# A graph layer with residual and layer norm on one core: GpSimd's statistics placed ahead of the next group's differences, one evacuation ahead of joins, three evacuations and four feature loads moved

## The chip, the core and the metric

The kernel runs on one core of a Trainium2 chip. The core has TensorE (PE, matrix multiply), VectorE (DVE), ScalarE (ACT), GpSimd (POOL) and SyncE (SP), which here only issues DMAs. Each engine works through its own queue in program order, and the queues meet at semaphores. The metric is device time of one launch in microseconds (us), the median of several runs; lower is better.

## The reference

```python
def _gcn_layer(x, adj, W, b):
    d_inv_sqrt = (jnp.sum(adj, axis=1) + 1e-09) ** (-0.5)
    msg = d_inv_sqrt[:, None] * adj * d_inv_sqrt[None, :] @ x
    return jax.nn.relu(msg @ W + b)
H_f = _gcn_layer(x, adj, W_f, b_f)            # x: 4096 x 128, adj: 4096 x 4096, fp32
H_s = _gcn_layer(spatial_x, adj, W_s, b_s)
attn = sigmoid(concat([H_f, H_s]) @ W_att + b_att)
x = x + attn * H_f + (1 - attn) * H_s
out = (x - mean(x)) / sqrt(var(x) + 1e-5)     # over the 128 features of a row
```

## The kernel before

Rows are cut into 32 tiles of 128; four tiles make a group, so there are 8 groups of output rows (512 each). The big product adj @ (D x) is taken in 64 items of four 128x512 blocks of the transposed adjacency (`raw`, 1 MB an item, three buffers; At is laid out on the host in the order of use). Each fp32 operand is split into a high and a low fp32r part: ACT writes the high part `Ah` (`high(k)`, L614), DVE the low part `Al` = raw - Ah (`low(k)`, L460), and likewise `Yh` (L642) and `Yl` (L471) for the scaled features. PE does three matmuls for a block and half (L377 to L379), 24 for an item, into one of four PSUM pairs; when a run of blocks ends, DVE evacuates the two halves of the pair into `acc` (`evacuate`, L479 or L482), and the next run on the same pair waits for that.

The degrees D need row sums of adj itself, which is loaded a second time in halves of 1 MB (`nat`, three buffers, `parts[k]` says before which item) and summed on ACT (L627); GpSimd turns sums into D (L723, L726) and, for the last two column groups, adds blocks of raw into column sums (L760). A load into `raw` waits for the low part three items back, one into `nat` for the row sum three halves back. SP issues all loads in one order written out by hand: for each item the halves of adj in `parts[k]`, the item's raw block, then feature loads (`load_x`, 0.5 MB each).

The last 16 items (FINAL = 48 to 63) end the product of one group after another: groups 0 to 6 end at items 50, 51, 53, 55, 57, 59 and 61, group 7 in two halves at 62 and 63. Each engine has the epilogue of a finished group at fixed items after its end (`L_MIX` 4, `L_JOIN` 5, `L_SQUARE` 6, `L_NORM` 7). For a group g:

- DVE evacuates it; PE multiplies it by the weights (`weigh(g)`, L387) behind the item after the group's last, and group 6 inside item 62;
- DVE `affine` (L496) and `logit` (L505); ACT `relu` (L649) and `gate` (sigmoid, L654);
- GpSimd `mix(r)` for each of the four tiles: the difference `fin` (L766) and residual plus H_s in `xs` (L767);
- DVE `join` (L513): xs += att * difference, with the row sum `ysum`;
- GpSimd `mean` (L772, `less`), ACT `square` (L658, with row sum `ysq`), GpSimd `deviation` (L777 vare, L780 rstd = power -0.5, L783 shift), ACT `normalise` (L663), SP stores the tile (L363).

On ACT, item k is: high(k), gate, normalise, square, relu, each where a group is due. On DVE it is: low(k), join, affine, logit, evacuations. Behind the loop both engines have the rest written out by hand. Group 7 goes in halves of two tiles (HALVES) with its statistics on DVE (`join_last`, `normalise_last`, L517 to L536) and the power on GpSimd (`last_deviation`, L788).

"Evacuation of 62" below is run 62, that is group 6; "high(63)" and "low(63)" are those of the last item. A count such as mix(1) or square(4) in the text is that of a group.

Of the kernel before, what the change touches and what calls it, by code (L numbers as in the profile page):

```python
# [13 lines left out]
GT = 4  # L14
# [53 lines left out]
def build(nc, At, adj, xs_in, W_f, W_s, b_f, b_s, W_att, b_att, out):  # L68
# [5 lines left out]
    G = T // GT  # L74
# [46 lines left out]
    FULL = (G - 2) * GT  # L121
    OWN_COLUMNS = 2 * G
    parts = {k: [] for k in range(K)}
    for k, r in [(0, 0), (1, 1), (4, 2), (5, 3), (8, 4), (9, 5), (10, 6), (11, 7)]:
        parts[k] = [2 * r, 2 * r + 1]
    for n, k in zip(range(16, 24), [13, 14, 15, 16, 16, 17, 17, 18]):
        parts[k].append(n)
    for n in range(24, 36):
# [18 lines left out]
        return sum(len(summed_blocks(i)) for i in range(k + 1))  # L147

    SHARED = [0, 1, 3]

    COLLECT = FINAL - 6

# [33 lines left out]
    with ExitStack() as ctx:  # L186
# [126 lines left out]
        @block.sync  # L313
        def _(sp):
            def load_item(k):
                if k >= RAWS:
                    sp.wait_ge(low_ok, GT * (k - RAWS + 1))
                    if summed_blocks(k - RAWS):
                        sp.wait_ge(block_sum_ok, blocks_summed(k - RAWS))
                if k == 1:  # L320
                    for i in range(GT):
                        sp.dma_start(raw[:, k, i * IB:(i + 1) * IB],
                                     At_v[k, :, i * IB:(i + 1) * IB]).then_inc(raw1_in[i], 16)
                else:
                    sp.dma_start(raw[:, k % RAWS, :], At_v[k]).then_inc(raw_in[k % RAWS], 16)

            def load_part(n):
                r = tile_of(n)
                if n >= NATS:
                    part_summed(sp, n - NATS)  # L330
                if r < FULL:
                    sp.dma_start(nat[:, n % NATS, :], adj_v[r, n % 2]).then_inc(nat_in[n % NATS], 16)
                else:
                    sp.dma_start(nat[:, n % NATS, :].rearrange("p (q c) -> p q c", q=2),
                                 adj_ends[r]).then_inc(nat_in[n % NATS], 16)

            def load_x(m):
                sp.dma_start(xs[:, m * GT:(m + 1) * GT, :], xs_v[m]).then_inc(xs_sem[m], 16)

            sp.dma_start(xs[:, 0:1, :], xs_v[0, :, 0:1, :]).then_inc(x_first, 16)  # L340
            for k in range(K):
                for n in parts[k]:
                    load_part(n)
                if k == 1:
                    sp.dma_start(xs[:, 1:GT, :], xs_v[0, :, 1:GT, :]).then_inc(xs_sem[0], 16)
                load_item(k)
                if k == 6:
                    load_x(1)
                if k % G == G - 1 and k // G + 2 < G:
                    load_x(k // G + 2)  # L350
                if k == 3 * G:
                    sp.dma_start(Wfs[:, 0:H], W_f).then_inc(const_in, 16)
                    sp.dma_start(Wfs[:, H:H2], W_s).then_inc(const_in, 16)
                    sp.dma_start(bias[:, 0:H], bf_v).then_inc(const_in, 16)
                    sp.dma_start(bias[:, H:H2], bs_v).then_inc(const_in, 16)
                    sp.dma_start(watt[:, :], watt_v).then_inc(const_in, 16)
                    sp.dma_start(batt[:, :], batt_v).then_inc(const_in, 16)
            for r in range(T):
                if r < LAST:
                    sp.wait_ge(norm_ok, r + 1)  # L360
                else:
                    sp.wait_ge(last_norm_ok, r - LAST + 1)
                sp.dma_start(out_v[r], xs[:, r, 0:F]).then_inc(stored, 16)  # L363
            sp.wait_ge(stored, 16 * T)
# [88 lines left out]
        def _(dve):  # L453
# [31 lines left out]
            def evacuate(e):  # L485
                evacuate_half(e, 0)
                evacuate_half(e, 1)
# [12 lines left out]
            def logit(r):  # L500
                dve.wait_ge(z_ok, r + 1)
                if r >= ZRING:
                    dve.wait_ge(logit_ok, r - ZRING + 1)
                c = (r % ZRING) * H2
                dve.scalar_tensor_tensor(out=nat[:, 1, c:c + H2], in0=z_of(r), scalar=0.0,  # L505
                                         in1=watt[:, :], op0=ALU.max, op1=ALU.mult,
                                         accum_out=lg[:, r:r + 1]).then_inc(logit_ok, 1)
# [25 lines left out]
            def normalise_last(r):  # L533
                dve.wait_ge(last_rstd_ok, r - LAST + 1)
                dve.tensor_scalar(xs[:, r, 0:F], xs[:, r, 0:F], mv[:, r, 0:1], rstd[:, r:r + 1],  # L535
                                  ALU.subtract, ALU.mult).then_inc(last_norm_ok, 1)  # L536

            def of_group(g):
                return range(g * GT, (g + 1) * GT)
# [10 lines left out]
            def evacuate_new(runs_ended):  # L550
                for e in runs_ended:
                    if e not in evacuated:
                        evacuated.add(e)
                        evacuate(e)

            for k in range(K):
                ended = [e for e in evac_order if end_item[e] == k - 2]
                evacuate_new(ended if k < 2 * G else ended[:1] if len(ended) == GT else [])
                if k == 1:
                    own_share(3)  # L560
                low(k)
                for r in y_at[k]:
                    if r >= PIECED:
                        y_low(r)
                g = group_at(k, L_JOIN)
                if g is not None:
                    for r in of_group(g):
                        join(r)
                g = group_at(k, L_MIX)
                if g is not None:  # L570
                    for r in of_group(g):
                        affine(r)
                    for r in of_group(g):
                        logit(r)
                if k < K - 1:
                    evacuate_new(ended)
            for r in of_group(TAIL - 2):
                join(r)
            evacuate(FIRST_LAST + TAIL - 1)
            evacuate_half(FIRST_LAST + TAIL, 0)  # L580
            for r in of_group(TAIL - 1):
                affine(r)
# [10 lines left out]
            for r in HALVES[0]:  # L593
                join_last(r)
            evacuate_half(FIRST_LAST + TAIL + 1, 1)
            for r in HALVES[0]:
                normalise_last(r)
            for r in HALVES[1]:
                affine(r)
                logit(r)  # L600
            for r in HALVES[1]:
                join_last(r)
            for r in HALVES[1]:
# [4 lines left out]
        def _(act):  # L608
# [47 lines left out]
            def square(r):  # L656
                act.wait_ge(less_ok, r + 1)
                act.activation(fin[:, r % ROWS, H_F], xs[:, r, 0:F], ACT.Square, bias=less[:, r:r + 1],  # L658
                               accum_out=ysq[:, r:r + 1]).then_inc(ysq_ok, 1)
# [6 lines left out]
            def of_group(g):  # L666
                return range(g * GT, (g + 1) * GT)

            for k in range(K):
                for n in parts[k]:  # L670
                    row_sum(n)
                high(k)
                if k == COLLECT + 3:
                    column_sums()
                for r in y_at[k]:
                    if r >= PIECED:
                        y_high(r)
                if k == FINAL:
                    act.wait_ge(const_in, 16 * 6)
                g = group_at(k, L_JOIN)  # L680
                if g is not None:
                    gate(of_group(g))
                g = group_at(k, L_NORM)
                if g is not None:
                    for r in of_group(g):
                        normalise(r)
                g = group_at(k, L_SQUARE)
                if g is not None and k < K - 1:
                    for r in of_group(g):
                        square(r)  # L690
                g = group_at(k, L_MIX)
                if g is not None:
                    for r in of_group(g):
                        relu(r)
            for r in of_group(TAIL - 3):
                square(r)
            gate(of_group(TAIL - 2))
            for r in of_group(TAIL - 3):
                normalise(r)
# [20 lines left out]
        def _(pool):  # L720
# [89 lines left out]
            def of_group(g):  # L810
                return range(g * GT, (g + 1) * GT)

            for g in range(TAIL):
                if g >= 1:
                    mean(of_group(g - 1))
                if g == TAIL - 1:
                    deviation(of_group(g - 1))
                for r in of_group(g):
                    mix(r)
                if 1 <= g < TAIL - 1:  # L820
                    deviation(of_group(g - 1))
            mean(of_group(TAIL - 1))
            for r in HALVES[0]:
                mix(r)
# [33 lines left out]
```

## Time and profile before

| | us |
|---|---|
| median of 3 runs | 418.4 (418.27 to 418.67) |
| the profiled execution's own time | 419.03 |
| its span (first to last instruction) | 417.2 |
| PE busy, share of the span | 375.0, 90% |
| DVE busy | 292.5, 70% |
| ACT busy | 284.5, 68% |
| GpSimd busy | 145.5, 35% |
| moved by DMA | 132.84 MB, 318 GB/s over the span |

PE has most of the span, but busy shares do not tell where time is lost. The rows below give start and length in us from the span's start; what stands in square brackets is how long the engine had been idle just before, and whose instruction ended that.

### The profile page before, as it was taken

The numbers are of one execution on the slowest core, as the hardware profiler recorded it, in microseconds if no ns is written. First come the engines' busy times: TensorE is split into PE (matmuls) and PEld (weight loads), VectorE is DVE, ScalarE is ACT, GpSimd is POOL, SyncE is SP. The second block draws the span as 40 slices with busy tenths as digits, with TensorE's granted clock in tenths as the row PEclk, the third lists the DMA queues.
The fourth block names the chain that finished last, engine by engine and source line by source line (L and its number), as shares of the span: only waits on it lengthen the run. The fifth ranks groups of instructions, "written<-read, shape, count | busy, mean of one in ns | idle before, by whom it ended". The sixth has DMA issues, their size and how long they took to land. (4 is left out here: it accounts for less than half of the span.)

```text
span 417.2 us, 5235 instructions
## 1 busy us (share of the span) xinstructions
PE 375.0 (90%) x1728; PEld 311.7 (75%) x1728; DVE 292.5 (70%) x407; ACT 284.5 (68%) x343; POOL 145.5 (35%) x194
## 2 busy tenths in 40 slices
PE   0679999689989998999989999999999999999492
PEld 0557887578868886888778877888888888887491
DVE  2569993496566966598654958489756996966776
ACT  3768588777887739877888677664433685574653
POOL 1203001000000791049211799342000557634574
PEclk9999999989999999999999999999999999999888
DMA  8999999999999989999999999897555535250001
GB/s 304 408 423 422 416 425 419 420 422 421 420 419 423 417 335 400 424 419 421 421 421 423 412 415 386 317 386 285 201 199 199 190 122 194 103 176 27 24 28 50
DMA packets 25530, 132.84 MB, mean 318 GB/s; under 512 B 2848, under 2 KB 7712, under 8 KB 11296
## 3 DMA queue, kind: packets, MB, share of 16 engines
q1 hardware_dynamic: 25504, 132.53, 79.4%
q8 instruction: 13, 0.21, 0.2%
q14 instruction: 13, 0.11, 0.1%
HBM read 130.42 MB, written 2.10 MB: 318 GB/s over the span
## 5 line engine op out<-in xcount | busy, mean ns | idle before, releaser
L377 PE MATMUL sums<-Ah,Yh 128*128 128x512 f32 (+1 forms) x528 | 206.0, 390 | 27.4 <-DVE Yl L471 18.8
L460 DVE TENSOR_TENSOR Al<-raw,Ah 128x2048 fp32r<-128x2048 f32 (+1 forms) x70 | 151.9, 2173 | 96.1 <-ACT Ah L614 95.1
L379 PE MATMUL sums<-Al,Yh 128*128 128x512 f32 (+1 forms) x528 | 204.0, 386 | 0.0
L378 PE MATMUL sums<-Ah,Yl 128*128 128x512 f32 (+1 forms) x528 | 203.9, 386 | 0.0
L614 ACT ACTIVATE Ah<-raw 128x2048 fp32r<-128x2048 f32 (+1 forms) x70 | 123.5, 1768 | 54.3 <-DMA raw<-in_At 29.0
L377 PEld LDWEIGHTS sums<-Ah,Yh 128*128 128x128 f32 x528 | 100.9, 191 | 50.4 <-DVE Yl L471 20.0
L627 ACT ACTIVATE nat<-nat 128x2048 f32<-128x2048 f32 x53 | 101.6, 1918 | 21.3 <-DMA nat<-in_adj 20.0
L379 PEld LDWEIGHTS sums<-Al,Yh 128*128 128x128 f32 x528 | 100.5, 190 | 19.7
L378 PEld LDWEIGHTS sums<-Ah,Yl 128*128 128x128 f32 x528 | 100.7, 191 | 19.1
L482 DVE TENSOR_TENSOR acc<-sums,acc 128x512 f32<-128x512 f32 (+1 forms) x114 | 71.8, 671 | 7.5 <-PE sums L379 7.3
L723 POOL TENSOR_SCALAR dg<-rs 128x1 f32<-128x1 f32 x22 | 11.3, 514 | 153.3 <-ACT nat L627 153.0
L760 POOL TENSOR_TENSOR S<-S,raw 128x512 f32<-128x512 f32 x32 | 58.6, 1832 | 8.2 <-DMA raw<-in_At 4.3
L766 POOL TENSOR_TENSOR fin<-fin 128x128 f32<-128x128 f32 x32 | 17.3, 541 | 64.7 <-ACT fin L649 64.7
L649 ACT ACTIVATE fin<-nat 128x256 f32<-128x256 f32 x32 | 12.6, 416 | 17.7 <-DVE nat L496 17.6
L387 PE MATMUL sums<-Wfs,acc 128*128 128x128 f32 x128 | 17.9, 296 | 6.9 <-DVE acc L482 6.8
L387 PEld LDWEIGHTS sums<-Wfs,acc 128*128 128x128 f32 x128 | 17.1, 209 | 8.1 <-DVE acc L482 7.7
L642 ACT ACTIVATE Yh<-xs,D 128x256 fp32r<-128x256 f32 x32 | 15.2, 494 | 11.1 <-POOL D L726 9.3
L663 ACT ACTIVATE xs<-xs,shift,rstd 128x128 f32<-128x128 f32 x28 | 11.5, 481 | 15.1 <-POOL shift L783 15.1
L471 DVE SCALAR_TENSOR_TENSOR Yl<-xs,D,Yh 128x256 fp32r<-128x256 f32 x32 | 18.4, 591 | 4.2 <-ACT Yh L642 4.2
L505 DVE SCALAR_TENSOR_TENSOR nat<-nat,watt 128x256 f32<-128x256 f32 x32 | 18.1, 614 | 0.1
L767 POOL TENSOR_TENSOR xs<-xs,fin 128x128 f32<-128x128 f32 x32 | 17.7, 553 | 0.0
L496 DVE SCALAR_TENSOR_TENSOR nat<-sums,D,bias 128x256 f32<-128x256 f32 x32 | 13.5, 475 | 2.9 <-PE sums L387 2.9
(45 smaller groups left out, 115.2 us busy)
## 6 DMA issues: line engine op xcount, KB each, us to landing
raw<-in_At SPq DMA_DIRECT2D x63, 1024.0 KB, 10.0
nat<-in_adj SPq DMA_DIRECT2D x56, 1024.0 KB, 11.5
xs<-in_xs SPq DMA_DIRECT2D x7, 512.0 KB, 11.2
out<-xs SPq DMA_DIRECT2D x32, 64.0 KB, 1.6
raw<-in_At SPq DMA_DIRECT2D x4, 256.0 KB, 9.7
xs<-in_xs SPq DMA_DIRECT2D x1, 384.0 KB, 9.2
xs<-in_xs SPq DMA_DIRECT2D x1, 128.0 KB, 2.4
watt<-in_W_att SPq DMA_DIRECT2D x1, 128.0 KB, 9.6
```

The lines of the kernel that those rows point to most:

```text
L377: pe.matmul(to, Yh[:, t % YRING, hs], high, start=first, stop=False)
L378: pe.matmul(to, Yl[:, t % YRING, hs], high, start=False, stop=False)
L379: mm = pe.matmul(to, Yh[:, t % YRING, hs], low, start=False, stop=last)
L387: return pe.matmul(sums[:, 3, bank, c + half * H:c + (half + 1) * H], acc[:, r // GT, half, q * P:(q + 1) * P], Wfs[:, half * H:(half + 1) ...
L460: dve.tensor_tensor(Al[:, k % SPLITS, a * IB:b * IB], raw[:, k % RAWS, a * IB:b * IB], Ah[:, k % SPLITS, a * IB:b * IB], ALU.subtract).the ...
L471: dve.scalar_tensor_tensor(out=Yl[:, r % YRING, :], in0=xs[:, r, :], scalar=D[:, r:r + 1], in1=Yh[:, r % YRING, :].bitcast(F32), op0=ALU.mult,
L482: dve.tensor_tensor(acc[:, g, half, a:b], sums[:, pair, half, 0:b - a], acc[:, g, half, a:b], ALU.add).then_inc(evac_ok, 1)
L505: dve.scalar_tensor_tensor(out=nat[:, 1, c:c + H2], in0=z_of(r), scalar=0.0, in1=watt[:, :], op0=ALU.max, op1=ALU.mult, accum_out=lg[:, r: ...
L614: act.activation(Ah[:, k % SPLITS, a * IB:b * IB], raw[:, k % RAWS, a * IB:b * IB], ACT.Copy).then_inc(high_ok, b - a)
L627: act.activation(nat[:, n % NATS, :], nat[:, n % NATS, :], ACT.Copy, accum_out=rs[:, r, h:h + 1]).then_inc(rs_act, 1)
L760: pool.tensor_tensor(S[:, g, :], S[:, g, :], raw[:, k % RAWS, j * IB:(j + 1) * IB], ALU.add).then_inc(block_sum_ok, 1)
L767: pool.tensor_tensor(xs[:, r, 0:F], xs[:, r, 0:F], f[:, H_S], ALU.add).then_inc(res_ok, 1)
```

## The change

Seven edits, none of which adds or drops an engine instruction:

1. SP and ACT: half 4 of adj is loaded and summed ahead of item 3, half 5 ahead of item 4 (both ahead of item 4 before).
2. SP: `load_x(2)` behind item 10 (was 7), `load_x(3)` behind 17 (15), `load_x(4)` behind 25 (23), `load_x(7)` behind 43 (47).
3. DVE: at items 17, 25 and 33 the run that ended two items earlier is evacuated ahead of the low part, not behind it.
4. DVE: the evacuation of 62 stands ahead of the joins of group 5.
5. DVE: `normalise_last` of the first half stands behind affine and logit of the second half.
6. ACT: the squares of group 4 stand in the loop at item 63, ahead of relu of group 5, not behind it.
7. GpSimd: `deviation(g-1)` stands ahead of `mix(g)` for all g, not only for g = 6.

(Edit 2 is four loads; the evacuations of edit 3 are of the runs that ended at items 15, 23 and 31.)

```diff
--- before.py
+++ after.py
@@ -121,8 +121,9 @@
     FULL = (G - 2) * GT
     OWN_COLUMNS = 2 * G
     parts = {k: [] for k in range(K)}
-    for k, r in [(0, 0), (1, 1), (4, 2), (5, 3), (8, 4), (9, 5), (10, 6), (11, 7)]:
+    for k, r in [(0, 0), (1, 1), (5, 3), (8, 4), (9, 5), (10, 6), (11, 7)]:
         parts[k] = [2 * r, 2 * r + 1]
+    parts[3], parts[4] = [4], [5]
     for n, k in zip(range(16, 24), [13, 14, 15, 16, 16, 17, 17, 18]):
         parts[k].append(n)
     for n in range(24, 36):
@@ -147,6 +148,8 @@
         return sum(len(summed_blocks(i)) for i in range(k + 1))
 
     SHARED = [0, 1, 3]
+    X_AFTER = {6: 1, 10: 2, 17: 3, 25: 4, 31: 5, 39: 6, 43: 7}
+    EVACUATE_FIRST = [k for k in range(K) if k < 2 * G or k in (17, 25, 33)]
 
     COLLECT = FINAL - 6
 
@@ -344,10 +347,8 @@
                 if k == 1:
                     sp.dma_start(xs[:, 1:GT, :], xs_v[0, :, 1:GT, :]).then_inc(xs_sem[0], 16)
                 load_item(k)
-                if k == 6:
-                    load_x(1)
-                if k % G == G - 1 and k // G + 2 < G:
-                    load_x(k // G + 2)
+                if k in X_AFTER:
+                    load_x(X_AFTER[k])
                 if k == 3 * G:
                     sp.dma_start(Wfs[:, 0:H], W_f).then_inc(const_in, 16)
                     sp.dma_start(Wfs[:, H:H2], W_s).then_inc(const_in, 16)
@@ -555,7 +556,7 @@
 
             for k in range(K):
                 ended = [e for e in evac_order if end_item[e] == k - 2]
-                evacuate_new(ended if k < 2 * G else ended[:1] if len(ended) == GT else [])
+                evacuate_new(ended if k in EVACUATE_FIRST else ended[:1] if len(ended) == GT else [])
                 if k == 1:
                     own_share(3)
                 low(k)
@@ -574,9 +575,9 @@
                         logit(r)
                 if k < K - 1:
                     evacuate_new(ended)
+            evacuate(FIRST_LAST + TAIL - 1)
             for r in of_group(TAIL - 2):
                 join(r)
-            evacuate(FIRST_LAST + TAIL - 1)
             evacuate_half(FIRST_LAST + TAIL, 0)
             for r in of_group(TAIL - 1):
                 affine(r)
@@ -593,11 +594,11 @@
             for r in HALVES[0]:
                 join_last(r)
             evacuate_half(FIRST_LAST + TAIL + 1, 1)
-            for r in HALVES[0]:
-                normalise_last(r)
             for r in HALVES[1]:
                 affine(r)
                 logit(r)
+            for r in HALVES[0]:
+                normalise_last(r)
             for r in HALVES[1]:
                 join_last(r)
             for r in HALVES[1]:
@@ -685,15 +686,13 @@
                     for r in of_group(g):
                         normalise(r)
                 g = group_at(k, L_SQUARE)
-                if g is not None and k < K - 1:
+                if g is not None:
                     for r in of_group(g):
                         square(r)
                 g = group_at(k, L_MIX)
                 if g is not None:
                     for r in of_group(g):
                         relu(r)
-            for r in of_group(TAIL - 3):
-                square(r)
             gate(of_group(TAIL - 2))
             for r in of_group(TAIL - 3):
                 normalise(r)
@@ -813,12 +812,9 @@
             for g in range(TAIL):
                 if g >= 1:
                     mean(of_group(g - 1))
-                if g == TAIL - 1:
                     deviation(of_group(g - 1))
                 for r in of_group(g):
                     mix(r)
-                if 1 <= g < TAIL - 1:
-                    deviation(of_group(g - 1))
             mean(of_group(TAIL - 1))
             for r in HALVES[0]:
                 mix(r)
```

## Rows read from the trace of the kernel before

**Rows 1.** Stretches: busy PE, PEld, DVE, ACT, POOL; clock, DMA share, GB/s.
```profile
160.00:250.00 90.00, 86.75 (x381) 70.84 (x379) 62.18 (x55) 72.99 (x65) 39.22 (x36) 1.00 1.01 420
290.00:350.00 60.00, 60.00 (x291) 50.58 (x290) 46.46 (x79) 31.89 (x50) 17.41 (x30) 1.00 0.52 187
```

**Rows 2.** PE's timeline (start, length, line; idle before), items 11, 16, 40.
```profile
84.58 0.50 PE L377 MATMUL sums<-Ah,Yh 128*128 128x512 f32 x1 [2.68 <-DVE Yl L471]
...
119.35 0.50 PE L377 MATMUL sums<-Ah,Yh 128*128 128x512 f32 x1 [1.58 <-DVE acc L482]
...
251.05 0.47 PE L377 MATMUL sums<-Ah,Yh 128*128 128x512 f32 x1 [1.38 <-issue]
```

**Rows 3.** ACT's and DVE's timeline ahead of item 40.
```profile
241.81 0.51 ACT L642 ACTIVATE Yh<-xs,D 128x256 fp32r<-128x256 f32 x1 [3.67 <-POOL D L726]
...
246.01 1.90 ACT L614 ACTIVATE Ah<-raw 128x2048 fp32r<-128x2048 f32 x1
...
248.05 2.90 DVE L460 TENSOR_TENSOR Al<-raw,Ah 128x2048 fp32r<-128x2048 f32 x1 [3.53 <-ACT Ah L614]
```

**Rows 4.** PE's timeline: the weights' products of groups 3, 5 and 6.
```profile
350.82 1.95 PE L387 MATMUL sums<-Wfs,acc 128*128 128x128 f32 x16
...
377.30 1.94 PE L387 MATMUL sums<-Wfs,acc 128*128 128x128 f32 x15 [0.96 <-DVE acc L482]
...
393.60 3.78 PE L387 MATMUL sums<-Wfs,acc 128*128 128x128 f32 x16 [5.88 <-DVE acc L482]
```

**Rows 5.** Stretches behind idle time of PE; clock behind POOL's count.
```profile
86.00:88.50 2.50, 2.50 (x8) 1.92 (x7) 2.50 (x4) 1.94 (x3) 0.00 (x0) 0.50 1.01 419
393.60:397.40 3.80, 3.80 (x18) 3.80 (x19) 1.16 (x3) 3.58 (x14) 0.52 (x2) 0.50 0.24 69
```

**Rows 6.** The list of waits (us in total, times, longest).
```profile
ACT xs L663 <- POOL shift L783: 15.1, 4, 4.3
```

**Rows 7.** ACT's timeline: normalise of group 3, high(63), normalise of group 4.
```profile
380.73 1.65 ACT L663 ACTIVATE xs<-xs,shift,rstd 128x128 f32<-128x128 f32 x4 [4.29 <-POOL shift L783]
382.29 1.90 ACT L614 ACTIVATE Ah<-raw 128x2048 fp32r<-128x2048 f32 x1
...
393.38 1.65 ACT L663 ACTIVATE xs<-xs,shift,rstd 128x128 f32<-128x128 f32 x4 [2.52 <-POOL shift L783]
```

**Rows 8.** DVE's timeline: low(57), evacuation, low(63), join, evacuation of 62, affine.
```profile
340.44 2.29 DVE L460 TENSOR_TENSOR Al<-raw,Ah 128x2048 fp32r<-128x2048 f32 x1 [0.88 <-ACT Ah L614]
...
346.37 1.28 DVE L482 TENSOR_TENSOR acc<-sums,acc 128x512 f32<-128x512 f32 x2
...
384.32 2.29 DVE L460 TENSOR_TENSOR Al<-raw,Ah 128x2048 fp32r<-128x2048 f32 x1 [3.75 <-ACT Ah L614]
...
390.90 0.44 DVE L513 SCALAR_TENSOR_TENSOR xs<-fin,att,xs 128x128 f32<-128x128 f32 x1 [0.42 <-ACT att L654]
...
392.27 1.61 DVE L482 TENSOR_TENSOR acc<-sums,acc 128x512 f32<-128x512 f32 x3
...
403.53 0.87 DVE L496 SCALAR_TENSOR_TENSOR nat<-sums,D,bias 128x256 f32<-128x256 f32 x2 [0.20 <-PE sums L387]
```

**Rows 9.** POOL's timeline: deviation of groups 0, 3 and 5, end of mix(6).
```profile
337.16 1.35 POOL L777 TENSOR_SCALAR vare<-ysq 128x4 f32<-128x4 f32 x1 [0.94 <-ACT fin L658]
...
377.50 2.87 POOL L780 TENSOR_TENSOR rstd<-vare,mhalf 128x4 f32<-128x4 f32 x1
...
396.73 0.20 POOL L777 TENSOR_SCALAR vare<-ysq 128x4 f32<-128x4 f32 x1 [3.23 <-ACT fin L658]
...
398.21 0.47 POOL L783 TENSOR_TENSOR shift<-less,rstd 128x4 f32<-128x4 f32 x1
...
402.12 0.51 POOL L767 TENSOR_TENSOR xs<-xs,fin 128x128 f32<-128x128 f32 x1
```

**Rows 10.** DVE's normalise_last of the first half; SP's last eight stores.
```profile
408.91 0.60 DVE L535 TENSOR_SCALAR xs<-xs,mv,rstd 128x128 f32<-128x128 f32 x2 [0.42 <-POOL rstd L788]
...
411.98 3.65 SPq L363 DMA_DIRECT2D out<-xs  x8
```

## The prediction, made before the changed kernel was run

> **What bounds the kernel now.** I read the table by stretches first. From 160 to 250 us DMA moves 420 GB/s with no slack (share 1.01) while PE is busy for 86.75 of 90 us; from 290 to 350 DMA moves 187 GB/s and PE is busy all the time [rows 1]. So there are two regimes: up to about item 40 the bytes set the pace and PE's pauses are its slack; from there PE sets it. PE's timeline shows those pauses: 2.68 us for Yl at item 11, 1.58 us for an evacuation inside item 16 (two more of that kind, 1.48 and 1.44 us, inside items 24 and 32), 1.38 us ahead of item 40 [rows 2]. Item 40 waited for its low part, 248.05 + 2.90 = 250.95, which waited for high(40) at 246.01, and ACT got to that late because it had waited 3.67 us for D ahead of two row sums [rows 3]. None of these waits is for PE. Third, the end: PE stands 0.96 us at the weights of group 5 and 5.88 us at those of group 6, both for an evacuation [rows 4], and runs at half clock behind the second (0.50, that is 1.2 GHz, from 393.6 to 397.4) [rows 5]. Why the evacuations are late is in ACT's rows: it waits four times, 15.1 us in all, for GpSimd's shift [rows 6]. One of these, 4.29 us, holds normalise of group 3 until 380.73, and high(63) stands behind it until 382.29 [rows 7], although item 60, whose buffer it takes, had ended at 377.30 - 0.96 = 376.34 [rows 4]. Low(63) follows at 384.32, then affine and logit of group 5, then its joins at 390.90, and only then, at 392.27, the evacuation of 62 [rows 8]. The whole end hangs on that shift.
>
> **Edits 1 to 3, up to item 40.** Edit 1 swaps a 1 MB half of adj with a 1 MB raw block on SP's queue; half 5, which gates D for tile 2, and raw 4 stay where they were. Raw 3 comes 1.25 to 2.5 us later (1 MB at 420 GB/s is 2.5 us), and DVE at that time has eight evacuation copies ahead of low(3), which cover it: zero; without that cover 2.5 us, absorbed below. Edit 2: load 2 no longer stands ahead of raw 8 to 10, so these come 0.5 MB / 420 GB/s = 1.25 us earlier, but it still stands ahead of raw 11, and PE's largest pause is at item 11: what is gained at 9 and 10 is waited for at 11. Loads 3 and 4 move two items and stay ahead of their first readers (items 20 and 28), load 7 is read at item 50. Load 7 goes into a stretch where DMA isn't full. Each costs SP one issue of 0.4 us, with nothing that starves behind it. Zero, bounds -0.7 to +0.3. Edit 3: the evacuation needs the end of the item before, and low(17) needs high(17), which is not there yet; so DVE does 1.28 us [rows 8] in idle time, and the three pauses of 1.58, 1.48 and 1.44 us go. That is 4.5 us at item 33. But the bytes ahead of raw 40 are the same, and the chain of rows 3 has no PE in it, so item 40 starts at 251.05 as before and PE waits there about 2.5 us in place of 1.38. Value: zero; bounds 4.5 us of gain (if item 40 did depend on PE) and 1.6 us of loss (rival 1).
>
> **Edits 4 to 7, the end; first the cost.** With deviation(0) ahead of mix(1), GpSimd waits for square(0), which is item 56's on ACT, though relu(1) was item 55's. DVE's join(1), at item 56 and ahead of low(57), now waits too. Vare of group 0 starts at 337.16 as before and takes 1.35 us; rstd and shift take what those of group 5 do, 398.68 - 396.93 = 1.75; so mix(1) starts near 340.3. A mix takes 402.63 - 398.68 = 3.95 us beside DVE's logits [rows 9] and, with DVE waiting, less; I take 3.4 to 3.95. The last join (0.34) ends at 344.0 to 344.6, and low(57) starts there rather than at 340.44. From there to the end of the evacuation of 59 was 347.65 - 340.44 = 7.2 us [rows 8], so it now ends at 351.2 to 351.8, and weigh(3), due at 350.82 [rows 4], waits 0.4 to 1.0 us. I take x = 0.6, below the middle since GpSimd isn't in mix(2) in the first part of these logits. Queued behind the waiting join: low(57), affine, logit, the load of raw 60; PE reads low(57) eight us later, so only weigh(3) feels it.
>
> **Then the gain.** For groups 2 to 5 square(g) stands just ahead of relu(g+1) on ACT, so GpSimd has its input by the time relu(g+1) is done, and the shift no longer waits for a mix (3.95 us) and a low part. The four waits of 15.1 us go, high(61), high(63) and what follows come as soon as PE frees the buffer, and the 0.96 us at weigh(5) go, which about pays for x. Step by step, with item 60 ending at 376.34 + x = 376.9:
> - high(63) starts at 377.0 instead of 382.29. From there to the end of logit of group 5 was 390.90 - 0.42 - 382.29 = 8.19 us: 385.2.
> - evacuation of 62 (edit 4), 1.28 us: 386.5. Item 61 ends near 384, so it isn't waited for. PE needs it at about 386.5 for weigh(6): the 5.88 us and the half clock go. PE is no longer what sets the end; DVE, ACT and GpSimd are.
> - joins of group 5, 1.2 to 1.44 us (392.34 - 390.90): 387.7. Mix(5) is done by then: square(4) now runs right behind high(63) (edit 6), deviation(4) ends near 383, mix(5) near 387.
> - mean(5), four squares and the hops: squares took 396.73 - (393.38 + 1.65) = 1.7 us, mean 0.2, hops 0.3: vare(5) at 389.9 instead of 396.73.
> - deviation(5) and mix(6): 402.63 - 396.73 = 5.9 us with two logits beside them, 5.3 without; 5.6: 395.5.
> - to affine of tile 28: 403.53 - 402.63 less the 0.20 us idle, 0.7: 396.2 instead of 403.53. That is 7.3 us.
> - from there the order is the old one, apart from edit 5: affine of tile 30 no longer waits behind 0.60 us of normalise_last; GpSimd sets the joins there, and what moves is the start of the last stores (SP has eight in 3.65 us [rows 10]) by 0 to 0.3 us; 0.2.
>
> Sum: 7.3 + 0.2 = 7.5 us less (x is in it). The profiled execution took 419.03 us, 1.8 us outside its span, so it would give 411.5; the median of the runs is 0.6 us under it: 418.4 - 7.5 = 410.9 us.
>
> **A rule that speaks against it.** Rstd of group 3 took 2.87 us beside low(62) and the joins behind it; that of group 5, with no low part near, at most 398.21 - 396.93 = 1.3 us [rows 9]. The Trainium skill (SBUF — State Buffer, Who interferes with whom) says that a VectorE instruction with two SBUF inputs contends with a GpSimd instruction that reads SBUF; rows and rule agree. By it every deviation that falls beside a low part is stretched to the low part's end. In the sum only deviation(4) could (low(63), 379.0 to 381.3): mix(5) would end up to 1.9 us later, 0.9 us of it past the evacuation and the join before it. That is the upper end of my own range, not a case.
>
> **Rivals.**
> 1. *The clock falls at item 40.* For: behind 2.68 us of idle PE ran at 0.50 for the stretch from 86.0 to 88.5 [rows 2, 5], and PE will stand 2.5 us ahead of item 40. Against: the 1.38 us there were followed by no such stretch, and 2.5 us is nearer to the other row only by length. A stretch of 2.5 to 3.8 us at half clock [rows 5] costs 1.2 to 1.9 us, 1.6 taken, with no slack behind: 412.5. The Trainium skill (TensorE: Matmul & The Clock Gate, HAM oscillation) describes such a fall behind idle gaps.
> 2. *The wait only moves.* Square(g) stands behind a high part on ACT; if that high part is late, the shift is late again, ACT waits as before, and only edit 4 is left: the joins and their wait, 392.27 - 390.48 = 1.8, with 0.2 and x: 418.4 - 1.8 - 0.2 + 0.6 = 417.0. Against: these high parts start when PE frees a buffer, and it does so in time.
> 3. *The middle gain arrives.* If raw 40 landed earlier, 4.5 us more: 406.4. Against: the full DMA of rows 1.
> 4. *Slower: the loop of a group is too long.* Mix(g+1) now needs join(g), so mean, squares, deviation, mix and join form a loop: 0.5 + 1.7 + 1.95 + 3.95 + 1.2 = 9.3 us, and PE gives a group (376.34 - 350.82) / 2 = 12.8 us. It decides from 3.5 us of waits for places in queues: a high part (1.9), a normalise (1.65) and a stretched rstd (1.9) make 14.75, 1.95 too long, in five groups 9.8 us: slower, 420.7. Against: these three rarely fall together.
>
> **Chances.** Forecast 0.63 (own range 409.5 to 412.0: x, contention, edit 5), rival 1 0.12, a part of the gain between it and rival 2 0.06 (413 to 416), rival 2 0.09, rival 3 0.05, rival 4 0.05. The range 408.8 to 414.8 leaves out rivals 2 to 4. A measurement of this kernel tells 0.2% (0.8 us) from no change. Faster by more than that: 0.93; within: 0.02 (between rivals 2 and 4); slower: 0.05.
>
> **What would show it.** Right: no idle PE inside items 16, 24, 32, about 2.5 us ahead of item 40 and its start at 251.05; weigh(3) 0.4 to 1 us late; no ACT wait for shift over 0.5 us from item 58 on; high(63) near 377, evacuation of 62 near 386, clock 1.00 from 386 to 398; affine of tile 28 near 396. Wrong: item 40 earlier by over 0.7 us, half clock behind it, or mix(6) ending past 397.

## Result and profile of the changed kernel

The changed kernel took 413.71 us (median of 4 runs, 412.51 to 414.65) against 418.33 us before (418.21 to 418.67) on the same chip: ratio 0.9887 [0.9858, 0.9915], 4.6 us less. The forecast was 410.9 us, range 408.8 to 414.8. So sign and range held and the size was 2.8 us too good; the time lies outside the 409.5 to 412.0 us to which the forecast itself had given 0.63, in the part between rivals 1 and 2 (413 to 416) that had 0.06. The profiled execution is the fastest of the four: 412.51 us, span 410.6 (the others 411.4 to 412.6). That of before had 417.2, while the median span of 23 further runs of before was 416.4. The comparison of the two profiles (6.6 us of span) therefore flatters the change by 1 us or more. All readings of one step below are from one profile each and good to a few tenths; sizes of whole edits go by the ratios.

The list of waits of the changed kernel (us in total, times, longest):

```profile
ACT fin L659 <- POOL less L771: 16.9, 5, 3.8
...
DVE xs L514 <- POOL xs L766: 8.9, 15, 2.5
...
ACT xs L664 <- POOL shift L782: 1.4, 2, 0.9
```

ACT's four waits for the shift, 15.1 us before [rows 6], are down to 1.4. In their place stand two new ones: ACT's squares wait 16.9 us for GpSimd's mean (`less`), and DVE's joins wait 8.9 us for GpSimd's mix. Most of that is off the path; the waits of the last groups are on it, as shown below.

PE's timeline: the pauses at items 36 and 40, the weights of groups 3, 5 and 6, and those of group 7.

```profile
227.07 0.47 PE L378 MATMUL sums<-Ah,Yh 128*128 128x512 f32 x1 [2.44 <-DVE acc L483]
...
250.70 0.47 PE L378 MATMUL sums<-Ah,Yh 128*128 128x512 f32 x1 [1.59 <-issue]
...
350.48 1.95 PE L388 MATMUL sums<-Wfs,acc 128*128 128x128 f32 x16
...
375.84 1.95 PE L388 MATMUL sums<-Wfs,acc 128*128 128x128 f32 x16
...
385.95 1.28 PE L388 MATMUL sums<-Wfs,acc 128*128 128x128 f32 x10
...
401.73 1.22 PE L388 MATMUL sums<-Wfs,acc 128*128 128x128 f32 x4 [1.89 <-DVE acc L483]
```

The three weights' products have no idle time ahead of them, where [rows 4] had 0.96 and 5.88 us. Item 40 starts at 250.70 (251.05 before, [rows 2]): 4.5 us of pauses inside items went and came back in front of items 33 (1.26 us), 36 (2.44) and 40 (1.59, before 1.38). Stretches of the same kernel (busy time of each engine, clock, DMA share, GB/s):

```profile
386.00:397.20 11.20, 11.20 (x96) 11.20 (x96) 6.99 (x31) 5.25 (x19) 7.80 (x19) 1.00 0.16 48
...
402.00:404.00 2.00, 0.95 (x4) 0.65 (x4) 1.37 (x5) 0.77 (x3) 1.72 (x5) 0.50 0.00 0
```

The half clock of [rows 5] behind weigh(6) is gone. PE ends its last item at 397.5 in place of 408.0, stands idle behind it and is at half clock (0.50, 1.2 GHz) for the last short products.

POOL's timeline: means of groups 1, 2 and 4, a mix of group 4, deviation(4), last mix(5), mean(5), vare(5), last mix(6).

```profile
342.82 2.12 POOL L771 TENSOR_TENSOR less<-ysum,share 128x4 f32<-128x4 f32 x1 [0.64 <-DVE xs L514]
...
354.88 2.12 POOL L771 TENSOR_TENSOR less<-ysum,share 128x4 f32<-128x4 f32 x1 [0.64 <-DVE xs L514]
...
374.01 2.51 POOL L766 TENSOR_TENSOR xs<-xs,fin 128x128 f32<-128x128 f32 x1
...
378.97 2.12 POOL L771 TENSOR_TENSOR less<-ysum,share 128x4 f32<-128x4 f32 x1 [0.64 <-DVE xs L514]
382.93 0.40 POOL L776 TENSOR_SCALAR vare<-ysq 128x4 f32<-128x4 f32 x1 [1.84 <-ACT fin L659]
...
384.63 0.20 POOL L782 TENSOR_TENSOR shift<-less,rstd 128x4 f32<-128x4 f32 x1
...
387.80 0.51 POOL L766 TENSOR_TENSOR xs<-xs,fin 128x128 f32<-128x128 f32 x1
388.94 0.20 POOL L771 TENSOR_TENSOR less<-ysum,share 128x4 f32<-128x4 f32 x1 [0.64 <-DVE xs L514]
390.99 0.44 POOL L776 TENSOR_SCALAR vare<-ysq 128x4 f32<-128x4 f32 x1 [1.85 <-ACT fin L659]
...
395.95 0.51 POOL L766 TENSOR_TENSOR xs<-xs,fin 128x128 f32<-128x128 f32 x1
```

The same 128x4 instruction takes 0.20 us at 388.94 and 2.12 us at 342.82, 354.88 and 378.97 (and at 366.93). ACT's timeline, high(63) and the first square of group 4; then DVE's: low(63), evacuation of 62, first and last join of group 5, affine of tile 28.

```profile
376.08 1.91 ACT L615 ACTIVATE Ah<-raw 128x2048 fp32r<-128x2048 f32 x1 [0.58 <-issue]
381.12 0.40 ACT L659 ACTIVATE fin<-xs,less 128x128 f32<-128x128 f32 x1 [3.13 <-POOL less L771]
```

```profile
378.74 2.29 DVE L461 TENSOR_TENSOR Al<-raw,Ah 128x2048 fp32r<-128x2048 f32 x1
...
383.89 1.28 DVE L483 TENSOR_TENSOR acc<-sums,acc 128x512 f32<-128x512 f32 x2
385.81 0.43 DVE L514 SCALAR_TENSOR_TENSOR xs<-fin,att,xs 128x128 f32<-128x128 f32 x1 [0.63 <-POOL xs L766]
...
388.44 0.35 DVE L514 SCALAR_TENSOR_TENSOR xs<-fin,att,xs 128x128 f32<-128x128 f32 x1 [0.45 <-POOL xs L766]
...
396.87 0.87 DVE L497 SCALAR_TENSOR_TENSOR nat<-sums,D,bias 128x256 f32<-128x256 f32 x2
```

The mean of group 4 lies inside low(63) (378.74 to 381.03) and ends with it, at 381.09. ACT had high(63) done at 378.0 and waits for the mean until 381.12. The evacuation of 62 ends at 385.17, but the joins behind it follow mix(5) tile by tile, 0.88 us each, and end at 388.79. So the mean is the one new piece on the path, and with it the mix of the group after it.

### The profile page after: what moved, and what is told of

It reads as the page before. It is cut to its first block and busy times, and to the rows that moved or that the text cites. A ratio compares the mean times of both kernels' runs of the same rounds, so it can differ in the third digit from the quotient of the medians.

```text
span 410.6 us, 5235 instructions
## 1 busy us (share of the span) xinstructions
PE 373.3 (91%) x1728; PEld 310.4 (76%) x1728; DVE 289.6 (71%) x407; ACT 282.7 (69%) x343; POOL 150.5 (37%) x194
## 5 line engine op out<-in xcount | busy, mean ns | idle before, releaser
L765 POOL TENSOR_TENSOR fin<-fin 128x128 f32<-128x128 f32 x32 | 15.3, 479 | 40.2 <-ACT fin L650 40.2
L659 ACT ACTIVATE fin<-xs,less 128x128 f32<-128x128 f32 x28 | 10.9, 390 | 16.9 <-POOL less L771 16.9
L766 POOL TENSOR_TENSOR xs<-xs,fin 128x128 f32<-128x128 f32 x32 | 22.3, 696 | 0.0
L388 PE MATMUL sums<-Wfs,acc 128*128 128x128 f32 x128 | 16.7, 282 | 3.5 <-DVE acc L483 3.5
L514 DVE SCALAR_TENSOR_TENSOR xs<-fin,att,xs 128x128 f32<-128x128 f32 x28 | 11.5, 421 | 11.4 <-POOL xs L766 8.9
L388 PEld LDWEIGHTS sums<-Wfs,acc 128*128 128x128 f32 x128 | 16.0, 195 | 4.4 <-DVE acc L483 2.1
L650 ACT ACTIVATE fin<-nat 128x256 f32<-128x256 f32 x32 | 11.4, 408 | 10.3 <-DVE nat L497 10.2
L497 DVE SCALAR_TENSOR_TENSOR nat<-sums,D,bias 128x256 f32<-128x256 f32 x32 | 13.4, 476 | 0.9 <-PE sums L388 0.9
```

The source lines that it names most:

```text
L388: return pe.matmul(sums[:, 3, bank, c + half * H:c + (half + 1) * H], acc[:, r // GT, half, q * P:(q + 1) * P], Wfs[:, half * H:(half + 1) ...
L765: pool.tensor_tensor(f[:, DIF], f[:, H_F], f[:, H_S], ALU.subtract).then_inc(dif_ok, 1)
L766: pool.tensor_tensor(xs[:, r, 0:F], xs[:, r, 0:F], f[:, H_S], ALU.add).then_inc(res_ok, 1)
```

## Experiments

Sizes in us are (1 - ratio) x 418.6. The ratio is to the runs of before on the same chip; three chips were used (e1 to e4, e5 to e8, e9 to e12), with medians of before of 418.57, 418.25 and 418.87 us. A ratio is estimated from all the runs and can differ a little from that of the two medians. A run's span is the time from its first to its last instruction, so it leaves out what comes before and behind; where spans tell another story than times, both are given.

| kernel | edits | median us | ratio [95%] |
|---|---|---|---|
| e1_tail_only | 4 to 7 | 412.95 | 0.9864 [0.9845, 0.9883] |
| e2_middle_only | 1 to 3 | 419.15 | 1.0016 [0.9999, 1.0032] |
| e3_after_again | all | 413.02 | 0.9861 [0.9840, 0.9882] |
| e4_deviation_behind | 1 to 6 | 418.55 | 0.9998 [0.9978, 1.0017] |
| e5_mean_on_act | 4 to 7, mean on ACT | 409.65 | 0.9791 [0.9771, 0.9811] |
| e6_tail_x7 | 4 to 7, load 7 of edit 2 | 413.12 | 0.9871 [0.9849, 0.9893] |
| e7_tail_evac_first | 3 to 7 | 412.44 | 0.9857 [0.9838, 0.9875] |
| e8_tail_loads | 4 to 7, 1, loads 2 to 4 of edit 2 | 411.93 | 0.9852 [0.9829, 0.9876] |
| e9_evac_swap_alone | 4 | 418.11 | 0.9982 [0.9972, 0.9992] |
| e10_squares_behind_relu | 4, 5, 7 | 414.29 | 0.9894 [0.9881, 0.9908] |
| e11_before_mean_on_act | none, mean on ACT | 419.03 | 1.0004 [0.9995, 1.0013] |
| e12_all_mean_on_act | all, mean on ACT | 410.58 | 0.9818 [0.9796, 0.9839] |

**Which half carries the gain.** The kernel before with edits 4 to 7 of the diff, then with edits 1 to 3, then the changed kernel once more.

> Edits 4 to 7 alone, on the kernel before (the order up to item 40 is the old one). Theory A (the gain is all in the end, and the two us by which runs of the changed kernel differ come from pauses of PE in the first 40 items, behind which the clock falls in some runs): 410.6 to 411.8 us in every run, spread under 0.6 us as before, item 40 at 251.0. Rival B (the spread comes from the end, from the order in which GpSimd and DVE take their shared port): median 413 to 414, spread 2 us as in the changed kernel. Rival C (edits 1 to 3 carry part of the gain): median above 413.7.

> Edits 1 to 3 alone, on the kernel before. Theory A: no gain, 418.3 at best and 420 in runs in which the clock falls at or behind item 33, 36 or 40; spread 1 to 2 us. Rival B: 418.0 to 418.5, spread under 0.5. Rival C: 415 to 417, item 40 clearly ahead of 250.

> The changed kernel once more, for its spread beside the two others. All theories: 412.5 to 414.7 us, median near 413.7.

The tail alone gives 5.7 us, all seven edits on the same chip 5.8 us, the middle alone -0.7 us with an interval that touches zero. So the whole gain is the tail's. The repeated kernel was 0.7 us quicker than in its first four runs, and before itself ranged from 417.89 to 420.87 in 23 runs: the changed kernel's scatter of 2 us isn't a property of the change. None of the three theories forecast e1 rightly: A had 410.6 to 411.8 us and B a spread of 2 us, the runs gave 412.95 with a spread of 0.3. In e2 A's runs near 420 came (417.69 to 420.84), but before has such runs too.

**Which edit of the tail.** e4 takes the changed kernel and puts the deviation back behind mix (edit 7 undone); e9 has edit 4 alone; e10 leaves edit 6 out of the tail.

```
 e4:              if g >= 1:
                      mean(of_group(g - 1))
+                 if g == TAIL - 1:
                      deviation(of_group(g - 1))
                  for r in of_group(g):
                      mix(r)
+                 if 1 <= g < TAIL - 1:
+                     deviation(of_group(g - 1))
```

> The changed kernel with edit 7 undone: deviation behind mix again, edits 1 to 6 kept. Theory A (the shift that comes late is what held high(61) and high(63)): the waits of ACT for shift are back, 4 us each; only edit 4 and the 0.2 us of edit 5 are left, 416 to 417 plus whatever the clock takes in the middle (0 to 1.6). Rival D (edits 4 and 6 carry the gain, edit 7 adds little): 411 to 413.5.

```
 e9, on before:
+            evacuate(FIRST_LAST + TAIL - 1)
             for r in of_group(TAIL - 2):
                 join(r)
-            evacuate(FIRST_LAST + TAIL - 1)
```

> Edit 4 alone on the kernel before. Theory L (the loop of GpSimd, joins and squares decides the end, and PE's wait for the weights of group 6 is not on the path once the joins wait for mix(5)): PE's pause ahead of weigh(6) shrinks by 1.3 to 1.9 us and nothing of it reaches the end, so the time is that of before within 0.5 us (417.9 to 418.8). Rival (the prediction's rival 2 priced this edit at 1.8 us on its own): 416.3 to 417.2.

```
 e10, on the tail:
-                if g is not None:
+                if g is not None and k < K - 1:
                     for r in of_group(g):
                         square(r)
 ...
+            for r in of_group(TAIL - 3):
+                square(r)
```

> Edits 4, 5 and 7 on the kernel before, edit 6 left out: the squares of group 4 again stand behind relu of group 5 on ACT. Theory L: relu(5) ends near 382.9, square(4) starts there in place of 381.0, and deviation(4), mix(5), the joins of group 5 and the end come 1.3 to 1.9 us later than with edit 6 (412.95): 414.2 to 414.9. Rival (edit 6 only reorders work that waits anyway): 412.7 to 413.4.

Without edit 7 nothing is left. Rival D (411 to 413.5 us) is excluded; theory A's 416 to 417, with up to 1.6 more, holds only at its upper edge (418.55). The parts add up: 0.75 us for edit 4 (e9) and 0.25 for edit 5 (below), less the 0.7 of e2, are 0.3, and e4 gives 0.1 with 0.8 on either side. ACT waits for shift as before; of its list of waits and its timeline:

```profile
ACT xs L664 <- POOL shift L782: 15.9, 5, 4.3
```

```profile
381.74 1.65 ACT L664 ACTIVATE xs<-xs,shift,rstd 128x128 f32<-128x128 f32 x4 [4.29 <-POOL shift L782]
```

This is the wait of [rows 7], 4.29 us to the hundredth. Edit 4 alone, PE's row of weigh(6) and DVE's of the affine behind the last join:

```profile
391.93 3.63 PE L387 MATMUL sums<-Wfs,acc 128*128 128x128 f32 x16 [4.00 <-DVE acc L482]
```

```profile
402.62 0.48 DVE L496 SCALAR_TENSOR_TENSOR nat<-sums,D,bias 128x256 f32<-128x256 f32 x1
```

PE's pause shrinks by 1.88 us (5.88 in [rows 4]) and the affine of tile 28, right behind the last join, comes 0.91 us earlier than in [rows 8], though this profile ran 0.2 us late from item 40 on (weigh(3) at 351.02, before 350.82); the runs give 0.75 us [0.3, 1.2]. Expected by the theory of the loop was no gain beyond 0.5 us; the measured one lies between that and the 1.8 us at which rival 2 of the prediction had priced the edit, nearer to the former. Edit 6 is worth the difference of e1 and e10, 0.0030 or 1.3 us (1.3 to 1.9 expected; the two are of different chips, and by median spans, each against before on its chip, it is 1.65). In e10 relu comes first, and the squares of group 4 stand behind it. Rows of ACT (relu) and POOL (vare(4)):

```profile
382.19 1.59 ACT L649 ACTIVATE fin<-nat 128x256 f32<-128x256 f32 x4 [3.46 <-DVE nat L496]
```

```profile
385.49 0.20 POOL L777 TENSOR_SCALAR vare<-ysq 128x4 f32<-128x4 f32 x1 [3.67 <-ACT fin L658]
```

In the changed kernel vare(4) is at 382.93. Of those 2.56 us 0.80 is e10's later item 40 (251.50 there, 250.70 here), so edit 6 moves it by 1.8.

**What the mean costs.** One 128x4 instruction a group goes from GpSimd to ACT, right ahead of the squares that read it; on the tail (e5), on before (e11) and on the changed kernel (e12).

```
+            def mean(rows):
+                a, b = rows[0], rows[-1] + 1
+                act.wait_ge(y_ok, b)
+                act.activation(less[:, a:b], ysum[:, a:b], ACT.Copy,
+                               scale=-1.0 / F).then_inc(less_ok, b - a)
             def square(r):
+                if r % GT == 0:
+                    mean(range(r, r + GT))
 ...
                 if g >= 1:
-                    mean(of_group(g - 1))
                     deviation(of_group(g - 1))
 ...
-            mean(of_group(TAIL - 1))
```

> Edits 4 to 7 alone, and the mean (less = -ysum/128, 128x4) of groups 0 to 6 computed by ACT ahead of its squares instead of by GpSimd. In the changed kernel GpSimd's mean of groups 1 to 4 takes 2.1 us instead of 0.2 beside a low part, and ACT's squares wait for it. Theory P (that wait is on the path of the end: square(4) to mix(5) to the joins of group 5): squares of group 4 start 1.6 us earlier, joins of group 5 end 1.3 to 1.8 us earlier, the whole 1.2 to 1.8 us faster than edits 4 to 7 alone (411.2 to 411.8 against 412.95; span 408.6 to 409.2 against 410.3). Rival (something else sets the end, the wait is slack): within 0.3 us of 412.95.

> The kernel before with the mean of groups 0 to 6 computed on ACT ahead of the squares. In before GpSimd's means took 0.20 us each, since the deviation ahead of them took the stretch (a vare of 2.2 or an rstd of 2.9 us). Theory P (what made the changed kernel's mean costly is its place beside the low part): no gain here, 417.9 to 418.6. Rival (handing the mean over between engines costs as such, in any order): at least 0.3 us for each of the last groups and for the end, 416.5 to 417.6.

> All seven edits with the mean of groups 0 to 6 on ACT. The same step with edits 4 to 7 alone gave 409.65. If edits 1 to 3 are worth nothing, 409.2 to 410.1; if they cost about 0.9 us, as the comparison of the middle alone with before would allow, 410.3 to 410.9; if they gain, under 409.2.

On the tail it brings 3.0 us more (0.9864 to 0.9791, on two chips; 2.55 by median spans, which are 6.05 us under before in e1 and 8.6 in e5), on before nothing (1.0004 [0.9995, 1.0013]; its 419.03 us lies above the 417.9 to 418.6 expected, as before itself had 418.87 on that chip). So it isn't the hand-over between engines that costs; it is the mean's place in the new order. Before, the deviation ahead of it took the stretch, and it still does in e11, where there is no mean on POOL:

```profile
377.50 2.87 POOL L787 TENSOR_TENSOR rstd<-vare,mhalf 128x4 f32<-128x4 f32 x1
```

In e5, ACT's mean and first square of group 4, POOL's vare(4) and first difference of mix(5), DVE's last join of group 5 and affine of tile 28:

```profile
377.46 0.19 ACT L659 ACTIVATE less<-ysum 128x4 f32<-128x4 f32 x1
377.68 0.41 ACT L665 ACTIVATE fin<-xs,less 128x128 f32<-128x128 f32 x1
```

```profile
379.49 0.54 POOL L782 TENSOR_SCALAR vare<-ysq 128x4 f32<-128x4 f32 x1 [4.44 <-ACT fin L665]
...
381.48 0.73 POOL L771 TENSOR_TENSOR fin<-fin 128x128 f32<-128x128 f32 x1
```

```profile
386.09 0.34 DVE L513 SCALAR_TENSOR_TENSOR xs<-fin,att,xs 128x128 f32<-128x128 f32 x1
...
394.20 0.87 DVE L496 SCALAR_TENSOR_TENSOR nat<-sums,D,bias 128x256 f32<-128x256 f32 x2
```

Squares(4) start 3.4 us earlier than in the changed kernel, mix(5) 3.3 us earlier, and the joins of group 5 no longer wait: they end at 386.43, 2.4 us earlier, and the affine of tile 28 comes 2.7 us earlier. Item 40 was 0.5 us earlier in this profile (250.23), so the profile gives 2.2 us where the ratios give 3.0 and the spans 2.55. I had expected 1.2 to 1.8 us. It was more because the stretch is in the loop over the groups and was lost in each: with the mean on POOL the loop comes round every 12.05 us (342.82, 354.88, 366.93, 378.97) with no wait for PE in it. In e5 join(4) was done at 376.02, while high(63) ran (375.64 to 377.55), and the mean and squares behind that waited for nothing. e5 and e12 beat both kernels; e5 is the best version found, 8.7 us less than before.

**Whether edits 1 to 3 cost.** e2 left a loss of 0.7 us possible. Each part was added to the tail alone.

```
 e6:  + if k == 43: load_x(7)        (not behind 47)
 e7:  + EVACUATE_FIRST = [k for k in range(K) if k < 2 * G or k in (17, 25, 33)]
 e8:  + parts[3], parts[4] = [4], [5]
      + X_AFTER = {6: 1, 10: 2, 17: 3, 25: 4, 31: 5, 39: 6, 47: 7}
```

> Edits 4 to 7 and of the middle only load 7, at item 43 instead of 47. The spans of kernels with edits 1 to 3 were about 0.9 us longer than of those without. Theory Q1 (load 7 takes the place of raw 44, whose slack was 0.7 us): span 411.0 to 411.5, item 44 late against item 40 by up to 1 us in some runs. Theories Q2, Q3 (below): 410.3, as edits 4 to 7 alone.

> Edits 4 to 7 and edit 3 (three evacuations ahead of low parts), no load moved. Theory Q2 (PE gets ahead, pauses longer ahead of items 33, 36 and 40, and the clock falls at 40 in some runs): span 411.0 to 411.5 in the median, some runs 1.6 us over the others. Q1 and Q3: 410.3. The part of the forecast that edit 3 is worth nothing: not below 410.0.

> Edits 4 to 7, edit 1 and loads 2 to 4 of edit 2; load 7 and the evacuations as before. Theory Q3 (the new order of loads costs DMA time ahead of raw 40): span 411.0 to 411.5, item 40 starts 0.5 to 1 us later than 250.6. Q1 and Q2: 410.3.

Ratios of 0.9871, 0.9857 and 0.9852 beside 0.9864 are -0.3, +0.3 and +0.5 us of gain, and each of the four ratios has an interval of 0.8 to 1.0 us on either side: no part stands out. Nor do the three theories hold. Q1: the spans of e6 have their median at 411.2 us, as Q1 had it, but in its profile item 40 was already late (251.14), ahead of the moved load, and from there to weigh(6) it takes 135.27 us (386.41 - 251.14) against 135.25 in e1 (385.85 - 250.60), so load 7 costs nothing there. Q2: the spans of e7 have 410.6, its runs lie within 0.6 us, and item 40 starts at 250.85. Q3: those of e8 have 410.1, and item 40 starts at 250.09.

Together the three edits cost 0.7 us in e2, -0.1 in e3 against e1, and 1.1 in e12 against e5 (two chips, intervals that overlap); e12's 410.58 us is where I had expected it if they cost 0.9. By median spans they cost 0.9 us (e2, 417.3 against 416.4), 0.85 (e3 against e1, 411.2 and 410.35, one chip) and 0.2 (e12 against e5, each against before on its chip). A step that the prediction's rival 1 had placed at item 40 did occur behind the pause at item 36, in e3, e4 and e7, three of the six profiles with edit 3. PE's timeline there in e3 and a stretch of it:

```profile
227.44 0.76 PE L378 MATMUL sums<-Ah,Yh 128*128 128x512 f32 x1 [2.42 <-DVE acc L483]
228.00 0.63 PE L379 MATMUL sums<-Ah,Yl 128*128 128x512 f32 x1
```

```profile
228.00:230.50 2.50, 2.50 (x7) 1.97 (x6) 1.79 (x1) 2.40 (x3) 0.00 (x0) 0.50 1.01 419
```

The clock fell to 0.50 behind 2.42 us of idle time, and matmuls took 0.63 us in place of 0.39. Item 40 started at 251.08 all the same, with 0.12 us of idle time ahead of it (the matmul before it ends at 250.96) and not 1.59: the fall ate slack. Item 40 started between 250.23 and 251.50 in the profiles of kernels with none of these edits, and between 250.70 and 251.44 with all three (e4 has the latest). From item 40 to weigh(6) the changed kernel and e3 take 135.25 us as e1 does, and e12 135.27, so what a profile could lose by these edits it would lose ahead of item 40. Their worth is zero to a loss of about 1 us; whether it is zero stays open, and no row shows a place where it is lost.

## Why the prediction was right or wrong

**What bounds the kernel** held. Up to item 40 the order of loads decides: item 40 was due at 251.05 and came between 250.70 and 251.44 in the five profiles of kernels with edits 1 to 3 (the changed kernel, e2, e3, e4 and e12). The pauses inside items 16, 24 and 32 went, and e2 gained nothing from that. Only the place where the time came back was named too narrowly: not 2.5 us ahead of item 40 alone, but 1.3 us at item 33, 2.4 at item 36 (an evacuation) and 1.6 at item 40. In the last third the whole gain hung on the shift, and e4 shows it: without edit 7 the ratio is 0.9998.

**x, the price of the cover at weigh(3), was zero and not 0.6 us.** Mix(1) began at 338.66, not near 340.3: vare(0) took 0.68 us where I had taken the 1.35 of [rows 9], the square was 0.6 earlier, and rstd and shift took 0.3 less. The last join ended at 342.60, and the evacuation of 59 at 349.03 rather than 351.2 to 351.8, since the logits ran with little GpSimd beside them. The bound of 0.4 us was thus too high; below it I had excluded zero without a reason.

**High(63) to evacuation of 62** came as worked out and a little sooner: 376.08 (377.0), end 385.17 (386.5). 0.35 us of that is the earlier item 40, 0.6 is x. The other 0.4 is a net of two things not in the sum: the logits took 0.42 us each (0.58 to 0.66 before, beside a mix), and low(63), now behind the late joins of group 4, began 2.66 us after high(63) instead of 2.03. Weigh(6) had no idle time ahead of it, and the clock stayed at 1.00 from 386 to 397.2.

**The step that failed is "mix(5) near 387, deviation(4) near 383, joins(5) at 387.7".** The shift of group 4 ended at 384.83 and the joins at 388.79. From the end of high(63) squares(4) were to run at once; they waited 3.1 us, 0.97 for the last join of group 4 and its hop, and 2.12 for the mean. I had priced mean(5) at 0.2 us, from its row in before, and mean(4) at nothing, without asking what stood beside it in the new place. The rule I had cited, the Trainium skill (SBUF — State Buffer, Who interferes with whom), fits the rows: every stretched instruction lies beside a low part (2.12 and 2.51 us in the rows above) and the same ones elsewhere take 0.20 and 0.51 or a little more. I had applied it to the deviation, which in the new order falls beside affine and logit (1.02 us for rstd in all groups), and not to the mean, which had taken the deviation's place beside the low part. And I had taken its worst case as 0.9 us at the end; e5 puts it at 2.2 to 3.0 us. Part of this error was hidden by luck: in e5 the joins of group 5 end 1.5 us behind the evacuation of 62, so here they could have ended near 386.7, 1.0 us ahead of the forecast, thanks to x and item 40; they ended 2.1 us behind that. None of the signs that I had named for a wrong forecast looked at the squares' wait, and none of them came.

**From there the sum held.** Joins to vare(5) 2.20 us (2.2 forecast), vare(5) to the end of mix(6) 5.47 (5.6), from there to the affine of tile 28 0.41 (0.7). So it came at 396.87 instead of 396.2. Edit 5's 0.2 us didn't show: from that affine to the end is 13.7 us in both profiles (417.2 - 403.53, 410.6 - 396.87). In e1 it is 13.45 (410.2 - 396.75) and in e4 and e5 13.4: there the last four short products ran at the higher clock. E9, without edit 5 and with the same quick products, has 13.7 as before. PE's row of e1 that answers to the last one of the changed kernel, 0.71 us in place of 1.22:

```profile
401.61 0.71 PE L387 MATMUL sums<-Wfs,acc 128*128 128x128 f32 x4 [1.88 <-DVE acc L482]
```

Affine of tile 30 waited 0.58 us for PE in e1 and 0.89 in the changed kernel; that 0.3 us, which the half clock takes, is about what the edit gives (0.25).

**The 2.8 us in terms of the sum.** 0.7 at the affine and 0.2 for edit 5 make the span 410.6 in place of 409.7; that execution took 412.51 rather than 411.5. The other 1.8 us is the base: I had taken the median as 0.6 us under the profiled execution, as it was before, and in the changed kernel it was 1.2 above. With e3 the changed kernel has 8 runs, from 412.01 to 414.65. The gain by ratios is 5.8 us (e3) and 4.7 us (first runs), against 7.5. With the mean off POOL e12 gives 7.6 us and e5 8.7: the forecast was that of a kernel in which the mean is not stretched.

**Rivals.** Rival 1 (half clock behind item 40) didn't come: PE stood 1.6 us there; where the fall came, behind the 2.4 us at item 36 in e3, e4 and e7, it met slack. Rival 2 is excluded by the list of waits, and e9 corrects its price for edit 4 from 1.8 to 0.75 us. Rival 3 is excluded by e2. Rival 4 was nearer than its 0.05: I had worked the loop out as 9.3 us, and the rows give 12.05, made up of 0.63 and 2.12 (last join and mean), 1.85 (squares), 1.84 (deviation) and 5.61 (mix, one instruction of it stretched to 2.51). PE gives a group (375.84 - 350.48) / 2 = 12.68 us. With over 0.63 us more in the loop every group would have lost time against PE.

## What to carry to other kernels

When a small instruction is moved, price it by what will stand beside it and not by its old row: here a stretch of 2 us stayed where it was in time and passed from the deviation to the mean. When work is reordered into a loop between engines, add the loop up with the stretched durations and compare it with the pace of the engine that feeds it. And an operation on four columns that two engines can do is worth trying on the one that needs its result next.

## What the runs showed of the hardware

- A GpSimd instruction on 128x4 elements took 0.20 us alone and 2.12 us when it began 0.2 us behind the start of a 128x2048 VectorE subtraction with two SBUF inputs; it ended 0.06 us behind the end of that subtraction (381.09 and 381.03). It is held to the end of the subtraction rather than slowed in proportion: `vare`, on 128x4 as well, began 0.31, 0.98 and 1.66 us into a low part, took 2.23, 1.35 and 0.68 us, and ended 0.05 to 0.06 us behind it each time. The rows, two pairs of before and one of the changed kernel:

```profile
336.18 2.28 DVE L460 TENSOR_TENSOR Al<-raw,Ah 128x2048 fp32r<-128x2048 f32 x1
337.16 1.35 POOL L777 TENSOR_SCALAR vare<-ysq 128x4 f32<-128x4 f32 x1 [0.94 <-ACT fin L658]
...
347.69 2.48 DVE L460 TENSOR_TENSOR Al<-raw,Ah 128x2048 fp32r<-128x2048 f32 x1
348.00 2.23 POOL L777 TENSOR_SCALAR vare<-ysq 128x4 f32<-128x4 f32 x1
```

```profile
334.87 2.28 DVE L461 TENSOR_TENSOR Al<-raw,Ah 128x2048 fp32r<-128x2048 f32 x1
336.53 0.68 POOL L776 TENSOR_SCALAR vare<-ysq 128x4 f32<-128x4 f32 x1 [5.39 <-ACT fin L659]
```

- Longer instructions end later behind the low part: an element-wise one of 128x128 (0.51 us by itself, 2.51 here) 0.32 us behind it (352.42 and 352.10), the 2.87 us `rstd` of before (1.02 by itself) 0.88 us (365.89 and 365.01). So what is added is the rest of the low part, about 2 us at most, whatever the instruction's own length.
- The clock of the last products was not settled by the pauses ahead of them: behind the same pauses of 1.64 to 1.67 and 1.88 to 1.89 us the last group of four took 0.71 us in e1 and e7 and 1.22 us in the changed kernel, e3, e6, e8 and e10. The granted clock of 401 to 403 was 0.81 in e1 and 0.50 in the changed kernel, and no edit tells these kernels apart (e3 is the changed kernel, e1 the tail alone, e6, e7 and e8 the tail with one or two further edits). The same at item 36: behind 2.39 to 2.44 us of idle time the clock fell to 0.50 in e3, e4 and e7 and stayed at 1.00 in the changed kernel, e2 and e12.
- Time outside the span was 1.74 to 1.95 us in two thirds of the runs and up to 3.5 us in the others; in three of the four runs of e1 it was 2.7 to 2.9. So kernels 0.2% apart need spans as well as times.
